# Four graph layers: layer 0's scores from rows of adj on VectorE, and adjT behind them into a ring of nine slots

## The reference, cut to what matters

```python
# layer 0
hw = h @ W
h_plus = (adj > 0) @ hw                 # no negative entries: h_minus is 0
e_plus = leaky_relu(h_plus @ a1); e_minus = leaky_relu(h_plus @ a2)
attn = softmax(where(adj > 0, e_plus[None, :], -9e15), axis=1)
x = norm(x + attn * adj @ hw)
# layer 1
A_t = adj + I;  D_inv = A_t.sum(1) ** -0.5
x = norm(x + relu(D_inv[:, None] * A_t * D_inv[None, :] @ (x @ W.T + b)))
# layers 2 and 3 use only few neighbours of each node:
# 2: softmax over neighbours with (1 - adj) * -1e9 added: the heaviest neighbour wins
# 3: sum over neighbours j of gelu(s_i + d_j + b) * adj_ij, then an update with two norms
```

## Time and profile before

| | |
|---|---|
| median of 3 runs | 719.37 us (717.54 to 721.62) |
| the profiled execution's own time, and its span | 716.03 us, 714.3 us |
| busy: PE, DVE, ACT, POOL | 455.7, 500.8, 301.7, 359.6 us |
| DMA | 119.98 MB, mean 168 GB/s |
| chain by engine | PE 36%, POOL 23%, DMA 17%, DVE 9%, issue 9% |
| mean granted clock of TensorE | 0.777 |

### The profile page before, as it was taken

One profiled execution on the slowest core, in us unless ns is written; L12 is line 12 of the kernel. 1 busy time (PEld: TensorE's weight loads), 2 busy tenths in 40 slices (PEclk: granted clock), 3 DMA queues, 4 the chain that ended last, 5 costly groups with the idle time before them and its releaser, 6 DMA issues.

```text
span 714.3 us, 6836 instructions
## 1 busy us (share of the span) xinstructions
PE 455.7 (64%) x1987; PEld 269.2 (38%) x1987; DVE 500.8 (70%) x1589; ACT 301.7 (42%) x363; POOL 359.6 (50%) x492
## 2 busy tenths in 40 slices
PE   5212113999987999999999447864543446447431
PEld 5112012444433556545435345543332234323220
DVE  2508922999893654798323566799999999998764
ACT  2566255445963332189954504013232332323331
POOL 7302640466663030476300174777777777777730
PEclk9555555699998999999999958966757776576555
DMA  8999996599992020279920223222222222222220
GB/s 332 347 426 423 373 429 147 197 405 411 392 382 82 0 79 1 96 283 387 426 78 16 67 53 100 52 51 59 52 59 59 59 59 53 59 59 59 52 48 7
DMA packets 32987, 119.98 MB, mean 168 GB/s; under 512 B 8550, under 2 KB 19668, under 8 KB 23924
## 3 DMA queue, kind: packets, MB, share of 16 engines
q1 hardware_dynamic: 20258, 80.99, 28.8%
q0 software_dynamic: 9952, 38.49, 17.1%
q10 hardware_dynamic: 2734, 0.01, 0.2%
HBM read 113.92 MB, written 5.55 MB: 167 GB/s over the span
## 4 chain that ended last, share of the span: by engine, by line
PE 36%; POOL 23%; DMA 17%; DVE 9%; issue 9%; ACT 3%; SPq 1%; ACTq 0%; POOLq 0%; DVEq 0%
PE ps L122 35%; POOL G L933 18%; DMA ring<-in_adjT_dram 15%; POOL Go L933 5%; ACT binT L1012 1%; DMA xT_s<-in_xT_dram 1%; DVE X L1711 1%; DVE agg L1851 1%; PE ps L1269 1%; PE ps L1275 1%; DVE st L1702 1%; DVE I L1515 1%; DVE G L1848 1%; SPq L836 1%; DVE V L1525 0%
## 5 line engine op out<-in xcount | busy, mean ns | idle before, releaser
L933 POOL DMA_INDIRECT G<-near,IX x147 | 142.5, 969 | 44.8 <-issue 44.8
L122 PE MATMUL ps<-ring,hwu 128*128 128x512 f32 (+3 forms) x264 | 114.6, 587 | 1.0 <-ACT hwu L1025 1.0
L122 PE MATMUL ps<-ring,xT_s 128*128 128x512 f32 (+2 forms) x264 | 106.9, 547 | 2.5 <-DMA ring<-in_adjT_dram 2.5
L1515 DVE FIND_INDEX8 I<-V,rows 128x8 uint32<-128x340 f32 (+2 forms) x176 | 88.1, 504 | 0.0
L1525 DVE MAX8 V<-rows 128x8 f32<-128x340 f32 (+2 forms) x176 | 85.5, 496 | 0.8
L122 PE MATMUL ps<-ident,agg 128*128 128x128 f32 (+1 forms) x44 | 14.6, 428 | 106.7 <-DVE agg L1851 106.7
L122 PE MATMUL ps<-E,M 128*128 128x321 f32 (+2 forms) x192 | 67.0, 510 | 16.7 <-DVE IO L1734 9.8
L122 PEld LDWEIGHTS ps<-ring,hwu 128*128 128x128 f32 (+1 forms) x264 | 51.1, 203 | 64.4 <-issue 63.2
L1012 ACT ACTIVATE binT<-ring 128x2708 bf16<-128x2708 f32 (+1 forms) x22 | 53.9, 2458 | 45.0 <-DMA ring<-in_adjT_dram 45.0
L956 POOL DMA_DIRECT2D rows<-in_adj_dram x18 | 10.9, 603 | 118.5 <-DVE I L1515 118.5
L122 PE MATMUL ps<-u,binT 128*128 128x4 bf16 (+1 forms) x484 | 18.1, 167 | 80.3 <-ACT binT L1012 80.3
(11 more groups left out here) (257 smaller groups left out, 835.9 us busy)
## 6 DMA issues: line engine op xcount, KB each, us to landing
ring<-in_adjT_dram SPq DMA_DIRECT2D x48, 1354.0 KB, 17.4
rows<-in_adj_dram POOLq DMA_DIRECT2D x17, 1354.0 KB, 10.1
rows<-in_adj_dram SPq DMA_DIRECT2D x4, 1354.0 KB, 23.6
G<-near,IX POOLq DMA_INDIRECT x147, 2.5
xT_s<-in_xT_dram SPq DMA_DIRECT2D x1, 1354.0 KB, 6.0
near<-hwu SPq DMA_DIRECT2D x1, 1344.0 KB
out_dram<-yo SPq DMA_DIRECT2D x21, 64.0 KB, 1.8
near2f<-hwu SPq DMA_DIRECT2D x5, 256.0 KB
```

Of the source, the lines that this page charges most:

```text
L122: return pe.matmul(dst, lhsT, rhs, start=start, stop=stop, skip_group_check=True)
L933: pool.indirect_dma_start(out=dst, out_offset=None, in_=table, in_offset=bass.IndirectOffsetOnAxis(ap=index, axis=0), engine_sem=o_g).then ...
L1515: return dve.max_index(I64[0:rn(n), n % 2, 8 * s:8 * s + 8], V64[0:rn(n), n % 2, 8 * s:8 * s + 8], segment(n, s))
```

## The change

The first pass goes over rows of adj. TensorE puts (x u) of all nodes, the same on all partitions, into PSUM (`wa_all` has u in each of its columns), and VectorE gets a block's scores in one instruction, (adj > 0) times that row, with the sum over columns taken along; ScalarE takes the row sums of the same block by a Relu with an accumulator. The 22 blocks come in the order of `ORDER`: the first two into `rows`, where they stay for the extraction, the last block (20 rows) third, the others through the ring, which has nine slots. All 22 blocks of adjT are then loaded behind them for layer 0, nine of them into slots as the scores and row sums let go of them, and layer 1 loads 13. No block is extracted before the scores are done; 10 blocks are extracted during layer 0 (`AHEAD` = 10) and 12 behind that. The neighbour counts come from the fourth column of `w3` with layer 0's denominators. The row sums are all there for layer 1's projection, so `scaled_late` goes. `TAIL1` is 5. `G3`, `E2` and `more` lie elsewhere in SBUF: `E2` in the slots from the fifth to the eighth, `more` where `rows` was. The gathers have no `engine_sem`.

```diff
-RING = 8
+RING = 9
 ROWS = 2
-EARLY = 4
-FIRST = 5
-AHEAD = 15
-LATE = 14
+AHEAD = 10
 TAIL = 7
-TAIL1 = 6
+TAIL1 = 5
...
+        ORDER = list(range(ROWS)) + [NB - 1] + list(range(ROWS, NB - 1))
+        RINGED = NB - ROWS
+        def slot(q):
+            return (NB - 1 + RINGED - q) % RING
+        def landed(q):
+            return 16 * (q // RING + 1)
+            return landed(RINGED + NB - 1 - j)
...
+        def in_pass(k):
+            n, q = ORDER[k], k - ROWS
+            if q < 0:
+                return n, rows[0:rn(n), k, 0:N], s_rows[k], 16
+            return n, ring[0:rn(n), slot(q), :], s_ring[slot(q)], landed(q)
...
-            def load_rows(n):
-                if n >= ROWS:
-                    sp.wait_ge(v_row, n - ROWS + 1)
-                sp.dma_start(rows[0:rn(n), n % ROWS, :], adj[n * P:n * P + rn(n), :]).then_inc(s_rows[n % ROWS], 16)
-            for j in range(NB):
-                if j >= RING:
-                    sp.wait_ge(c_sg, j - RING + 1)
-                load_ring(j)
-                if j in (1, 4, 9, 13):
-                    load_rows((1, 4, 9, 13).index(j))
-                if j == NB - 8:
+            for k in range(NB):
+                n, at, landing, _ = in_pass(k)
+                if k >= ROWS + RING:
+                    sp.wait_ge(v_score, k - RING + 1)
+                    sp.wait_ge(c_rs, k - RING + 1)
+                sp.dma_start(at, adj[n * P:n * P + rn(n), :]).then_inc(landing, 16)
+                if k == ROWS + RING:
                     sp.wait_ge(c_hw, 8)
                     sp.dma_start(bass.AP(near0.tensor, 0, [[D, P], [P * D, NB - 1], [1, D]]), hwu[:, 0:NB - 1, 0:D]).then_inc(s_near, 16)
                     sp.dma_start(near0[P * (NB - 1):N, :], hwu[0:LAST, NB - 1, 0:D]).then_inc(s_near, 16)
-            sp.dma_start(X[:, 0:NB - 1, :], bass.AP(x.tensor, 0, [[D, P], [P * D, NB - 1], [1, D]])).then_inc(s_xl, 16)
-            sp.dma_start(X[0:LAST, NB - 1, :], x[P * (NB - 1):N, :]).then_inc(s_xl, 16)
-            for p in range(NB - RING):
-                sp.wait_ge(p_l0, p + 1)
-                sp.wait_ge(c_sg, NB + p + 1)
-                load_ring(NB - RING - 1 - p)
+            for p in range(NB):
+                if p < RING:
+                    sp.wait_ge(v_score, NB + p - RING + 1)
+                    sp.wait_ge(c_rs, NB + p - RING + 1)
+                else:
+                    sp.wait_ge(p_l0, p - RING + 1)
+                    sp.wait_ge(c_sg, p - RING + 1)
+                load_ring(NB - 1 - p)
+                if p == RING - 1:
+                    sp.wait_ge(v_xz, 1)
+                    sp.dma_start(X[:, 0:NB - 1, :], bass.AP(x.tensor, 0, [[D, P], [P * D, NB - 1], [1, D]])).then_inc(s_xl, 16)
+                    sp.dma_start(X[0:LAST, NB - 1, :], x[P * (NB - 1):N, :]).then_inc(s_xl, 16)
...
-            def all_begun(so_far):
-                if so_far:
-                    pool.wait_ge(o_g, so_far)
             def gather(dst, table, index, signal):
                 pool.indirect_dma_start(out=dst, out_offset=None, in_=table,
-                                        in_offset=bass.IndirectOffsetOnAxis(ap=index, axis=0), engine_sem=o_g).then_inc(signal, 16)
+                                        in_offset=bass.IndirectOffsetOnAxis(ap=index, axis=0)).then_inc(signal, 16)
...
-                if n + ROWS < EARLY:
-                    pool.wait_ge(v_pos, n + 1)
-                elif n + ROWS < NB:
+                if n + ROWS < NB:
                     pool.wait_ge(v_row, n + 1)
                     pool.dma_start(rows[0:rn(n + ROWS), n % ROWS, :],
                                    adj[(n + ROWS) * P:(n + ROWS) * P + rn(n + ROWS), :]).then_inc(s_later[n % ROWS], 16)
-                    pool.wait_ge(v_pos, n + 1)
-                else:
-                    pool.wait_ge(v_pos, n + 1)
+                pool.wait_ge(v_pos, n + 1)
...
-            for j in range(NB):
-                act.wait_ge(s_ring[j % RING], in_first(j))
-                if j >= 2:
-                    act.wait_ge(p_e, j - 1)
-                act.activation(binT[0:rn(j), j % 2, :], ring[0:rn(j), j % RING, :], ACT.Sign).then_inc(c_sg, 1)
-            act.dma_start(diag[:, 0:NB - 1], bass.AP(adj.tensor, 0, [[N + 1, P], [P * (N + 1), NB - 1], [1, 1]]),
-                          allow_slow_non_contiguous=True).then_inc(s_diag, 16)
-            act.dma_start(diag[0:LAST, NB - 1:NB], bass.AP(adj.tensor, P * (NB - 1) * (N + 1), [[N + 1, LAST], [1, 1]]),
-                          allow_slow_non_contiguous=True).then_inc(s_diag, 16)
+            for k in range(NB):
+                n, at, landing, count = in_pass(k)
+                if k:
+                    act.wait_ge(c_rs, k)
+                act.wait_ge(landing, count)
+                act.activation(xT_s[0:rn(n), 0:N], at, ACT.Relu, accum_out=dinv[0:rn(n), 0, n:n + 1]).then_inc(c_rs, 1)
+                if k == 4:
+                    act.dma_start(diag[:, 0:NB - 1], bass.AP(adj.tensor, 0, [[N + 1, P], [P * (N + 1), NB - 1], [1, 1]]),
+                                  allow_slow_non_contiguous=True).then_inc(s_diag, 16)
+                    act.dma_start(diag[0:LAST, NB - 1:NB], bass.AP(adj.tensor, P * (NB - 1) * (N + 1), [[N + 1, LAST], [1, 1]]),
+                                  allow_slow_non_contiguous=True).then_inc(s_diag, 16)
...
-                act.wait_ge(v_rs, 2)
+                act.wait_ge(v_rs, 1)
                 for q, n in enumerate(blocks_of(c)):
-                    scale = dinv[0:rn(n), 1, n:n + 1] if n < AHEAD else 1.0
-                    last = act.activation(hw1[0:rn(n), n, :], bank(c, q * D, D)[0:rn(n), :], ACT.Copy, scale=scale)
-                last.then_inc(c_hw1, 1)
-            def scaled_late():
-                act.wait_ge(v_rs, 3)
-                act.activation(dinv[:, 0, AHEAD:NB], dinv[:, 0, AHEAD:NB], ACT.Sqrt, bias=ones[:, 0:1]).then_inc(c_dinv, 1)
-                act.wait_ge(v_rs, 4)
-                act.wait_ge(c_hw1, CH)
-                for n in range(AHEAD, NB):
-                    last = act.activation(hw1[0:rn(n), n, :], hw1[0:rn(n), n, :], ACT.Copy, scale=dinv[0:rn(n), 1, n:n + 1])
+                    last = act.activation(hw1[0:rn(n), n, :], bank(c, q * D, D)[0:rn(n), :], ACT.Copy, scale=dinv[0:rn(n), 1, n:n + 1])
...
-                    act.wait_ge(v_rs, 1)
-                    act.activation(dinv[:, 0, 0:AHEAD], dinv[:, 0, 0:AHEAD], ACT.Sqrt, bias=ones[:, 0:1]).then_inc(c_dinv, 1)
+                    act.wait_ge(c_rs, NB)
+                    act.activation(dinv[:, 0, :], dinv[:, 0, :], ACT.Sqrt, bias=ones[:, 0:1]).then_inc(c_dinv, 1)
...
+            for at, m in chunks:
+                last = mm(pe, ps[:, at:at + m], wa_all[:, :], xT_s[:, at:at + m], True, True)
+            last.then_inc(p_u, 1)
...
-            zeros = w3[:, 0:4, :].rearrange("p n w -> p (n w)")
-            mm(pe, bank(0, 0, 4 * NB), zeros, zeros[:, 0:4 * NB], True, False)
-            pe.wait_ge(v_u3, 1)
-            for j in range(NB):
-                pe.wait_ge(c_sg, j + 1)
-                for i in range(NB):
-                    last = mm(pe, bank(0, 4 * i, 4)[0:rn(i), :], binT[0:rn(j), j % 2, i * P:i * P + rn(i)], u3[0:rn(j), j, :], False, j == NB - 1)
-                last.then_inc(p_e if j < NB - 1 else p_ecol, 1)
-                if j == 8:
+            pe.wait_ge(c_hw, 8)
...
-                if j == AHEAD:
-                    pe.wait_ge(c_hw1, CH + 1)
...
+            dve.tensor_scalar(wa_all[:, :], ones[:, :], wa_s[:, 0:1], None, ALU.mult).then_inc(v_wa, 1)
-            dve.wait_ge(c_hw, 8)
-            few.done(dve.tensor_copy(u3[:, :, 0], hwu[:, :, D]))
-            few.done(dve.tensor_tensor(uf[:, 0, :], hwu[:, :, D], u3[:, :, 0], ALU.subtract))
-            few.done(dve.tensor_copy(u3[:, :, 1], uf[:, 0, :]))
-            few.done(dve.tensor_tensor(uf[:, 1, :], uf[:, 0, :], u3[:, :, 1], ALU.subtract))
-            dve.tensor_copy(u3[:, :, 2], uf[:, 1, :]).then_inc(v_u3, 1)
+            u_all = ps[:, 0:N]
+            unused = X[:, :, :].rearrange("p n d -> p (n d)")[:, 0:N]
+            def scores(k):
+                n, at, landing, count = in_pass(k)
+                r = rn(n)
+                if k:
+                    dve.wait_ge(v_score, k)
+                if n == NB - 1:
+                    few.done(dve.tensor_copy(zd[:, n, 0:1], zd[:, 0, 0:1]))
+                dve.wait_ge(landing, count)
+                dve.scalar_tensor_tensor(out=unused[0:r, :], in0=at, scalar=0.0, in1=u_all[0:r, :], op0=ALU.is_gt, op1=ALU.mult,
+                                         accum_out=zd[0:r, n, 0:1]).then_inc(v_score, 1)
+            dve.wait_ge(p_u, 1)
+            for k in range(NB):
+                scores(k)
+                if k == NB - 6:
+                    folded_weights()
...
-            extract(0, BLOCK)
-            extract(BLOCK, FIRST * BLOCK)
-            dve.wait_ge(p_ecol, 1)
-            quads = bank(0, 0, 4 * NB).rearrange("p (n w) -> p n w", w=4)
```

(23 more changed lines are left out.)

98 lines of the change are left out of this document (45 added, 53 removed).

## The result

The changed kernel takes 731.75 us (median of 4 runs, 731.2 to 732.3) beside 718.45 us for the kernel before on the same chip: ratio 1.018, 95% interval 1.014 to 1.023. It is slower by 1.8%. (Every ratio here leaves out the runs that lie over 1.5% above the fastest one of their kernel: two of e7's six, one of the kernel before beside it.) The profiled execution took 732.0 us, its span 730.2; that of the kernel before, 716.0 and 714.3, was the shortest of its runs. Ahead of the gathers, the last write into `E2` (from `more`, VectorE) starts at 423.1 us in place of 408.6, 14.6 us later; what lies behind it takes 307.1 us in place of 305.7.

What follows compares the result with a forecast made beforehand. It took loads to bound the first pass, TensorE layers 0 and 1, VectorE mostly the gathers; VectorE's extraction would end late. 716.0 us + 6.6 = 722.6, with 3.4 for the median 726.0 us; range 709 to 742.

Steps and rivals of the forecast that it cites:

- First pass: Scores over adj: loads pace them at 3.24 us each, scores end at 91.3 us, layer 0 starts 27.6 us earlier.
- Layer 0: TensorE waits 13 us for adjT; 56 loads, 77.6 MB, land by 196 us and the tail begins at 199.5 us.
- The ten last blocks: VectorE's extraction behind layer 0's tail start: ends 167 us after it, at 366.6 us in place of 337.4.
- 2 us for late row loads: Extraction behind the tail's start: delay by row loads landing late beside ring loads, 2 us in all, bounds 0 and 18.
- The other terms: From tail's start: 74 us to the second block's end, 1.7 for an extra block, 1 for TensorE's clock, 88.4 for ten blocks.
- the starving case: Rival, extraction: each late block takes 11.3 us, 16 us more in all, 742 us; chance 0.14.
- The rule on queues: Skill's rule that DMA engines alternate between GpSimd's and SP's queues: row loads land in some 7 us, making the 2 us 0.
- The 2.3 us back: Layer 1: TensorE runs up to two chunks ahead and TAIL1 of 5 shortens later chunks, so 8.9 us later becomes 6.6.
- The rest: Removed small operations, late scaling, moved buffers and the gathers' lost increment: counted as nothing.
- half rate: Rival, first pass: two f32 SBUF sources halve VectorE's throughput, scores 5.9 us a block, 765 us; chance 0.03.
- the gap: Rival, gathers: the 0.30 us between gathers goes with its increment, 25 us of up to 41 come back, 701 us; chance 0.06.
- Keeping up: Rival, layer 0: loads land by 183 us at 422 GB/s, tail begins at 187 us, 711 us in all; chance 0.19.

Runs made afterwards that it cites:

- e7: Changed kernel with AHEAD 12 in place of 10 and the extraction pieces behind the tail's chunks laid as 3, 3, 4, 5, 8, 3: ratio to before 0.986.
- e9: Changed kernel without near0's write of 21 blocks and the wait for it: ratio to the kernel before 1.008.
- e12: Changed kernel with AHEAD 12, pieces 3, 3, 4, 5, 8, 3, and diag's loads issued by GpSimd instead of ScalarE: 711.87 us, ratio to before 0.991.
- e3: Changed kernel loading only a quarter of each row block from block 2 on, general path off, output not the reference's: ratio to before 0.985.
- e4: Changed kernel loading only a quarter of row blocks 14 to 21, general path off, output not the reference's: ratio to before 1.012.
- e5: The changed kernel itself, unchanged, run again on another chip as a control: ratio to the kernel before 1.015.
- e1: Changed kernel with AHEAD 12 in place of 10, two more blocks extracted before layer 0's results: ratio to the kernel before 0.993.
- e6: Changed kernel with AHEAD 12 in place of 10, a repeat on another chip: ratio to the kernel before 0.995.
- e8: Changed kernel with u copied from PSUM to SBUF, from which all 22 scores read it: ratio to the kernel before 1.016.
- e2: Changed kernel with AHEAD 14 in place of 10, four more blocks extracted before layer 0's results: ratio to the kernel before 0.998.
- e10: Changed kernel with ScalarE's issue of diag's loads moved ahead of everything on its queue: ratio to the kernel before 1.036.

## Why the prediction was right, and where its terms were off

The forecast was 726.0 us and slower; measured are 731.75. The mechanism was the forecast's: an earlier first pass, layer 0 held by the bytes of the rows' second reading and of all 22 blocks of adjT, VectorE with too many blocks left, its slack of 18.9 us used up. The size was not: on the profiled execution's own time the forecast was +6.6 us and the trace shows +16.0. That the medians lie closer (5.8 us) is luck. The forecast added 3.4 us because the profiled run of the kernel before lay that far below the median; the changed kernel's lies 0.3 above its own. The difference of 9.4 us, step by step:

- **First pass.** Forecast: scores at 91.3 us, 3.0 us each, one landing in 3.24 us. Measured: 93.9, 2.975, and 3.3 between undisturbed scores. The write of near0 was counted as one load, 3.24 us; the wait behind it was 5.3 us, and e9 without it ends at 91.5. ScalarE's function was said to hide because 2.46 is below 3.24; the issue of diag's loads between the functions was not counted, a DMA that I had passed over. It cost nothing that shows (e12's scores end at 94.8 us without it).
- **Layer 0.** Forecast: 77.6 MB by the last landing at 196 us, the tail at 199.5. The windows sum to 306 x 25 + 400 x 40 + 395 x 30 + 411 x 50 + 394 x 54.3 (to 199.3 us) = 77.4 MB: the count of bytes was right, the rate in the first pass was not, 395 to 400 GB/s where 422 was taken. By 104 us that makes 39.2 MB in place of 41.0, 4.5 us at 401 GB/s. The rate from there on is that 401, where 398 was taken, which gives 0.7 back, 0.2 MB fewer give 0.5, and the last landing is 3.3 us late. e9 shows that near0's write weighs more than the one load that it was counted as. TensorE's wait and its cause came as forecast, and e3 shows that it goes with the rows.
- **The ten last blocks.** 167 us from the tail's start to the end of the extraction, 169.0 measured (202.6 to 371.6). The term "2 us for late row loads" was the one mis-sized: e4 takes the late ones out and gets 5.0 us back. With two buffers a load goes out when a block is done and is due one block later: in these rows of two blocks one waits, and a pair takes 8.7 + 10.35 us, 0.8 us more for each block than without the wait. Beside the ring's loads of layer 1 that happened twice, and one block more took 11.3 us. The forecast saw the 10.1 us landing beside the 8.85 us block and still took the value of the undisturbed blocks, which ended ahead of most of the ring's loads. The other terms (74, 1.7, 1 and 88.4) were high by 1 us together. The upper bound of that term was mis-added: eight blocks at 11.3 less 8.85 us are 19.6 us, not 18, and the starving case 744 us, not 742.
- **The rule on queues.** The forecast had set it aside because the measured landing of 10.1 us contradicts a landing in 7; the kernel after shows 10.9 us, and a VectorE that waits for row loads. To let the measurement decide was right; the 2 us then taken for it were too few.
- **The 2.3 us back.** They didn't come. From VectorE's first result of layer 1 to E2's last write 38.65 us passed, where it was 37.77: 0.9 lost, not 2.3 won, 3.2 us of the miss. TensorE ran two chunks ahead, as said, then waited 8.9 us for VectorE's X, and came back at a lower clock: from 385 to 395 us the granted clock is 0.59 (0.50 in e5), where it is 1.00 in the kernel before and in e1 0.84, with the levels of 1.2 and 2.4 GHz at 0.50 and 1.00. The same part takes 35.5 us in e1, 35.6 in e12, 36.8 in e6 and e7, and 37.7 in e5, so a us or so is spread between traces. The forecast gave no working for its 2.3, and it forgot that the engine ahead waits, and comes back at the lower level. That the clock ate the 2.3 is argued from these rows, not shown by a run, and TAIL1 was not tried alone.
- **The rest.** 1.4 us longer behind E2's last write, not in the sum. The gather's gap stays at 0.30 us (44.8 us in 147) without the increment: the 0 taken for it was right.

Together: 3.1 + 2.0 + 3.2 + 1.4 = 9.7, less 0.3 in the steps behind the last places (12.8 us in place of 13.1). Of the rivals, half rate is refuted by the 2.975 us of the changed kernel itself and by e8 even for two sources in SBUF, and the gap by its row. Keeping up is refuted by the windows: it needed 422 GB/s, from the start at that, while the forecast's own first 25 us had 308; with these its landing is at 191 us, not 183. Starving was half right: blocks of 10.35 us, every second one, and a single one of 11.3, not 11.3 in each.

## What to carry to other kernels

Where a change reads a matrix once more, count every load up to the last landing and set it against the rate of a stretch that has the same mix of loads: here 395 to 400 GB/s where near0's rows and diag's elements or waits for slots were among them, 422 in the kernel before (25 to 65 us), without. Which of them lowers it was not taken apart. Look then at where the DMA engines are left empty (here 212 to 240 us) and at which engine waits just ahead of that, for work can be moved there at no cost: one constant, AHEAD from 10 to 12, turned 1.5% slower (e5) into 0.6% faster (e1, e6). With two buffers, a landing that is longer than the work (10.9 against 8.7 us) delayed every second block here; blocks that ran ahead of the other queue's loads say nothing on it. And once VectorE is out of the way, the last landing isn't the end: TensorE's 14 products behind it took 11.1 us in e7 and 6.9 in e2, by how long TensorE had waited ahead of them.

## What the hardware showed beyond this

- Behind a load of 4-byte elements (diag, 2,688 of them) the engine that issues the next DMA of the same queue was held: ScalarE for 17.65 us in the changed kernel, 22.1 in e9 and 38.7 in e10, and it started no activation meanwhile. SyncE was held 20.6 us behind near0's 512-byte rows and 27.4 us behind X's, the first of these 6.9 us in e10, so it isn't a fixed price. From GpSimd diag's pair took 2.05 us (e12).
- scalar_tensor_tensor over 2708 f32 columns, with an accumulator: 2975 ns with a source in PSUM, 2979 ns with both in SBUF.
- A row load of GpSimd beside SyncE's ring loads lands in 10.9 us in the median, where its bytes are 3.4 us at 411 GB/s. A quarter of it took 6.9 us (e3).
